# A graph network on one core: roots turned on TensorE, slots made early, a first strip by groups, and a loop of two blocks

## What is computed

```python
# part 1, over the edges (row = src, col = dst)
h = concatenate([x[row], x[col], edge_attr]) @ W1 + b1
h = relu((h - mean(h)) * rsqrt(var(h) + 1e-5) * gamma + beta)     # statistics over the edges
out = segment_sum(h @ W2 + b2, row) / (counts + 1) + x
x = layernorm(x + out)
# part 2
deg = segment_sum(1, dst with self loops);  dinv = rsqrt(deg);  norm = dinv[src] * dinv[dst]
conv = lambda h, W, b: segment_sum((h @ W)[src] * norm, dst) + b
h = relu(conv(x, W0, b0)); h = relu(conv(h, W1, b1))
x = layernorm(x + conv(h, W2, b2))
```

## Time and profile before

| | |
|---|---|
| median of 3 runs | 3832.4 us (3830.92 to 3836.69) |
| profiled execution | 3838.11 us, span 3836.3 us, mean granted clock 0.983 |
| TensorE busy | 3620.9 us (94%), matmuls x40721 |
| VectorE busy | 2525.0 us (66%) |
| ScalarE busy | 1489.2 us (39%) |
| GpSimd busy | 967.4 us (25%) |
| chain that ended last | PE 65%, DVE 24%, issue 8%, SPq 2%, ACT 1%, DMA 1% |

### The profile page before, as it was taken

One profiled execution on the slowest core, in us unless ns is written; L12 is line 12 of the kernel. 1 busy time (PEld: TensorE's weight loads), 2 busy tenths in 40 slices (PEclk: granted clock), 3 DMA queues, 4 the chain that ended last, 5 costly groups with the idle time before them and its releaser, 6 DMA issues.

```text
span 3836.3 us, 104225 instructions
## 1 busy us (share of the span) xinstructions
PE 3620.9 (94%) x40721; PEld 2589.0 (67%) x40942; DVE 2525.0 (66%) x3757; ACT 1489.2 (39%) x3772; POOL 967.4 (25%) x890
## 2 busy tenths in 40 slices
PE   4699999999998799999999999997999999999999
PEld 3488888888887677777777777774444444454444
DVE  6899999999995689888989889973111111111112
ACT  5355555455453366666666666662000000000000
POOL 0001000000101467766767677610000000000000
PEclk8899999999999999999999999998999999999999
DMA  7222322322334755555555555544666566656664
GB/s 239 55 88 84 102 86 84 102 87 84 100 88 146 125 162 158 157 155 151 161 158 157 147 158 158 157 137 153 193 200 195 193 195 200 193 189 208 209 209 132
DMA packets 435059, 571.31 MB, mean 149 GB/s; under 512 B 200059, under 2 KB 359684, under 8 KB 427940
## 3 DMA queue, kind: packets, MB, share of 16 engines
q1 hardware_dynamic: 403140, 510.29, 43.6%
q0 software_dynamic: 25088, 51.43, 5.0%
q10 hardware_dynamic: 6624, 6.42, 0.5%
HBM read 458.48 MB, written 109.53 MB: 148 GB/s over the span
## 4 chain that ended last, share of the span: by engine, by line
PE 65%; DVE 24%; issue 8%; SPq 2%; ACT 1%; DMA 1%; DVEq 0%; ACTq 0%
PE py L1654 30%; PE ph L1358 11%; PE pSum L1375 10%; DVE prod_raw L1145 8%; PE ph L1361 7%; DVE ring_raw L1118 6%; PE ph L1353 3%; DVE q L1154 1%; DVE q L1171 1%; DVE q L1167 1%; PE pY L854 1%; DVE q L1168 1%; DVE rank L1178 1%; DVE q L1173 1%; PE pbk L915 1%
## 5 line engine op out<-in xcount | busy, mean ns | idle before, releaser
L1308 POOL DMA_INDIRECT q<-pq_dram,chosen x784 | 851.4, 1086 | 405.3 <-ACT ph L1411 204.1
L1654 PE MATMUL py<-ring_raw,p 128*128 128x512 bf16 (+1 forms) x3822 | 784.7, 368 | 18.0 <-DVE dummy L1814 16.1
L1358 PE MATMUL ph<-p,prod_raw 128*128 (+1 forms) x7056 | 685.3, 220 | 22.7 <-DVE prod_raw L1501 12.2
L1654 PEld LDWEIGHTS py<-ring_raw,p 128*128 128x128 bf16 x3822 | 362.3, 98 | 432.1 <-DVE dummy L1814 16.5
L1358 PEld LDWEIGHTS ph<-p,prod_raw 128*128 128x128 bf16 x7056 | 493.7, 98 | 122.6 <-issue 4.8
L1418 ACT ACTIVATE x<-ph 128x512 bf16<-128x512 f32 x588 | 351.3, 597 | 464.6 <-PE ph L1361 334.6
L1361 PE MATMUL ph<-q,prod_raw 128*128 128x128 bf16 x4704 | 522.4, 220 | 0.0
L1375 PE MATMUL pSum<-x,ring_raw 128*128 128x384 bf16 x2401 | 500.4, 328 | 4.9 <-DVE x L1519 4.9
L854 PE MATMUL pY<-p,ring_raw 128*128 128x128 bf16 x7203 | 502.5, 219 | 0.3 <-issue 0.3
L1514 DVE SCALAR_TENSOR_TENSOR ring_raw<-ph,x 128x512 f32<-128x512 f32 x588 | 403.9, 687 | 132.5 <-ACT x L1418 126.5
L1830 DVE TENSOR_TENSOR yt<-py,dinv_row 128x512 f32<-128x512 f32 (+1 forms) x39 | 25.8, 661 | 696.6 <-PE py L1654 696.6
(11 more groups left out here) (334 smaller groups left out, 4372.5 us busy)
## 6 DMA issues: line engine op xcount, KB each, us to landing
ring_raw<-at_dram SPq DMA_DIRECT2D x252, 896.0 KB, 4.8
at_dram<-ring_raw SPq DMA_DIRECT2D x49, 1568.0 KB, 5.7
prod_raw<-lrow_dram SPq DMA_DIRECT2D x147, 384.0 KB
prod_raw<-lrow_dram SPq DMA_DIRECT2D x196, 256.0 KB
prod_raw<-lrow_dram SPq DMA_DIRECT2D x49, 416.0 KB
q<-pq_dram,chosen POOLq DMA_INDIRECT x784
arow_dram<-x SPq DMA_DIRECT2D x294, 36.8 KB
x<-arow_dram SPq DMA_DIRECT2D x147, 54.0 KB
```

Source lines behind the costliest of these rows:

```text
L1308: nc.gpsimd.indirect_dma_start(q_rows[i][:, k, :], None, pq_rows, bass.IndirectOffsetOnAxis(ap=chosen[u][:, i, k:k + 1], axis=0)).then_inc ...
L1358: last = nc.tensor.matmul(bank[:, k * P:(k + 1) * P], T[q][:, 0, at:at + P], p_b[:, :, m3, :].rearrange("p a d -> p (a d)"), start=False, ...
L1654: last = nc.tensor.matmul(py[par][:, 0:w], g3[c % 2][:, 7 * i + m, k, :], ring[i][:, 0:w // P, m, :], start=i == m == k == 0, stop=i == m ...
```

## The change

Four edits, all in stages two and three:

1. SyncE no longer writes `dinv_col` to DRAM element by element. TensorE transposes it (behind the statistics, after `dinv_made`) into `pSum[0]`, ScalarE copies that to `dinv_rows` behind the root of the variance (`dinv_kept`), and SyncE writes 49 rows of 512 B, now behind the three loads of x. TensorE waits for `dinv_kept` ahead of the first `sums`.
2. `quarter` is split into `targets` (L1501) and `slots` (L1508). The four `slots(0, k)` now stand ahead of VectorE's wait for `square_used`, the four `targets(0, k)` behind the bound.
3. Every strip takes its chunks in the order 4, 5, 0, 1, 2, 3, 6. TensorE begins the first strip when VectorE has read group 11 (`cg_taken` 12, the last in the py banks), and waits ahead of each chunk for the groups whose blocks it reads; `third` signals `node_done` for each group.
4. TensorE's source loop has 2 blocks in its body instead of 16.

```diff
+CHUNKS = (4, 5, 0, 1, 2, 3, 6)
@@ sp_2
                     for k in range(4):
                         quarter(0, k)
-                    put(sp, S["dinv_made"], 1)
-                    sp.dma_start(dinv_dram.rearrange("a (b p) -> p (a b)", p=P), dinv_col[:], ...).then_inc(S["dinv_out"], 16)
                     for u in range(3):
                         sp.dma_start(fl(xg[u][:]), t["xT"][:, u * 512:(u + 1) * 512]).then_inc(S["x_in"], 16)
+                    put(sp, S["dinv_kept"], 1)
+                    sp.dma_start(dinv_dram.rearrange("a (b p) -> (a b) p", p=P), dinv_rows[0:B, :]).then_inc(S["dinv_out"], 16)
@@ pe_2
                     nc.tensor.matmul(st[:, D:2 * D], ones_f[0:3, :], xs[0:3, D:2 * D], start=False, stop=True).then_inc(S["stats_made"], 1)
+                    pe.wait_ge(S["dinv_made"], 1)
+                    nc.tensor.transpose(pSum[0][0:B, 0:D], dinv_col[:], ident_f[:]).then_inc(S["dinv_turned"], 1)
@@ pe_2, sums
+                        if isinstance(b, int) and b == g == 0:
+                            pe.wait_ge(S["dinv_kept"], 1)
                         pe.wait_ge(S["z_low"], b * 13 + (g + 1))
@@ pe_2
-                    each_block(pe, one_block, 16)
+                    each_block(pe, one_block, 2)
@@ act_2
                     nc.scalar.activation(bt[1][:], bt[0][:], ACT.Sqrt).then_inc(S["bn_rooted"], 1)
+                    act.wait_ge(S["dinv_turned"], 1)
+                    nc.scalar.activation(dinv_rows[0:B, :], pSum[0][0:B, 0:D], ACT.Copy).then_inc(S["dinv_kept"], 1)
@@ dve_2
+                    def quarter(b, k):
+                        targets(b, k)
+                        slots(b, k)
...
+                    for k in range(4):
+                        slots(0, k)
                     dve.wait_ge(S["square_used"], 7)
@@ dve_2
                     for k in range(4):
-                        quarter(0, k)
+                        targets(0, k)
                     one_block(0, 0, False)
@@ sp_3, strip_loads
-                    for i in range(7):
-                        put(sp, S["chunk_used"], (j + 13 * c) * 7 + i + 1)
+                    for n, i in enumerate(CHUNKS):
+                        put(sp, S["chunk_used"], (j + 13 * c) * 7 + n + 1)
                         chunk(i, j, w)
@@ pe_3
-                pe.wait_ge(S["credits3"], 1)
+                pe.wait_ge(S["cg_taken"], 12)
@@ pe_3, strip
-                    for i in range(7):
+                    for at, i in enumerate(CHUNKS):
                         pe.wait_ge(a_in[i], (n + 1) * 16)
+                        if isinstance(j, int) and c == j == 0:
+                            pe.wait_ge(S["node_done"], (7 * i + 6) // 4 + 1)
...
-                        if i == 1 and has_tail:
+                        if at == 1 and has_tail:
                             tail(c, n - 1, 4)
                 for c in range(3):
-                    pe.wait_ge(S["g_taken"], 13 * c + 1)
+                    if c:
+                        pe.wait_ge(S["g_taken"], 13 * c + 1)
                     strip(c, 0, c % 2, STRIP, False)
@@ dve_3
                 def third(j):
...
-                    return V.tensor_tensor(g3[0][:, 4 * j:4 * j + nb, 2, :], gb[:, 0:nb, :], g3[0][:, 4 * j:4 * j + nb, 1, :], ALU.subtract)
+                    V.tensor_tensor(g3[0][:, 4 * j:4 * j + nb, 2, :], gb[:, 0:nb, :], g3[0][:, 4 * j:4 * j + nb, 1, :], ALU.subtract).then_inc(S["node_done"], 1)
...
-                last.then_inc(S["node_done"], 1)
-                dve.wait_ge(S["node_done"], 1)
+                dve.wait_ge(S["node_done"], 13)
```

More of the change, by code:

```diff
@@ L575, in build @@
         S.update({n: fit_sem(n) for n in """phase2 rows_set quad_summed dv2 moments_in squared square_used weighed stats_made bn_sqrt bn_rooted bound_ready credits t_ready hf_ready
-             mm_done z_hi z_res z_mid z_low sum_done sum_taken credits3 node_done dinv_made dinv_out dinv_in s_turned s_copied s_made cg_taken c_squared x1_made ga_made g_hi g_res g_mid x_rest0 x_rest1
+             mm_done z_hi z_res z_mid z_low sum_done sum_taken credits3 node_done dinv_made dinv_turned dinv_kept dinv_out dinv_in s_turned s_copied s_made cg_taken c_squared x1_made ga_made g_hi g_res g_mid x_rest0 x_rest1
              chunk_used y_taken yt_ready tail_done ln_ask ln_root out_ready out_sent dv3 root_b x_in bias_done g_taken rows_chosen q_put bank_open""".split()})
@@ L1228, in build @@
                 psq = [x1_free[:, u * 7 * D:(u + 1) * 7 * D].rearrange("p (j d) -> p j d", d=D) for u in range(2)]
-                s_raw = sb("s_raw", [P, D])
+                s_raw = sb("s_raw", [P, D]); dinv_rows = sb("dinv_rows", [P, D])
                 wvb = sb("wvb", [P, 4, D], BF16); neg_g = sb("neg_g", [P, D]); bt = [sb(f"bt{u}", [P, D]) for u in range(4)]
@@ L1462, in dve_2, with targets, slots @@
                     link(V.scalar_tensor_tensor(out=s_raw[:], in0=wa[:, 1, :], scalar=a2_all[:, 4:5], in1=qa[:], op0=ALU.mult, op1=ALU.add))
+                    def quarter(b, k):
+                        targets(b, k)
+                        slots(b, k)
+                    def targets(b, k):
+                        dve.wait_ge(t_in[k], b * T_IN[k] + T_IN[k])
+                        places = T[k].rearrange("p f s -> p (f s)")[:, 0:(QCELLS[k] + len(TCELLS[k])) * P]
+                        V.tensor_scalar(places, places, pid1[:, 0:1], None, ALU.is_equal).then_inc(S["t_ready"], 1)
+                    def slots(b, k):
+                        if not (isinstance(b, int) and b == 0):
+                            dve.wait_ge(S["sum_done"], b * 13 + (QUARTERS[k][1] - 13))
+                        dims = [P, PAIRS[k], P, 2]
+                        cols = slice(4 * QUARTERS[k][0], 4 * QUARTERS[k][0] + 2 * PAIRS[k])
+                        own = lo_all[:, b:b + 1, cols] if isinstance(b, int) else lo_all[:, bass.ds(b, 1), cols]
+                        own = own.rearrange("p a (g u) -> p (a g) u", u=2).unsqueeze(2)
+                        V.tensor_tensor(hotf[k], iota_lo[:].unsqueeze(1).to_broadcast(dims), own.to_broadcast(dims), ALU.is_equal).then_inc(S["hf_ready"], 1)
+                    for k in range(4):
+                        slots(0, k)
                     dve.wait_ge(S["square_used"], 7)
@@ L1496, in dve_2 @@
                     last.then_inc(S["bound_ready"], 1)
[L1498 to L1508, removed]
                     def left(b, g):
@@ L1599, in pool_3 @@
             def pool_3(pool):
-                pool.wait_ge(S["node_done"], 1)
+                pool.wait_ge(S["node_done"], 13)
             def pe_3(pe):
@@ L1654, in strip @@
                                 last = nc.tensor.matmul(py[par][:, 0:w], g3[c % 2][:, 7 * i + m, k, :], ring[i][:, 0:w // P, m, :],
-                                                        start=i == m == k == 0, stop=i == m == 6 and k == 2)
+                                                        start=at == m == k == 0, stop=at == m == 6 and k == 2)
                         last.then_inc(S["chunk_used"], 1)
-                        if i == 1 and has_tail:
+                        if at == 1 and has_tail:
                             tail(c, n - 1, 4)
                 for c in range(3):
-                    pe.wait_ge(S["g_taken"], 13 * c + 1)
+                    if c:
+                        pe.wait_ge(S["g_taken"], 13 * c + 1)
                     strip(c, 0, c % 2, STRIP, False)
@@ L1804, in dve_3 @@
                     if 0 <= s - 2:
-                        last = third(s - 2)
+                        third(s - 2)
                     if 0 <= s - 1 < 13:
                         scaled(s - 1)
-                last.then_inc(S["node_done"], 1)
-                dve.wait_ge(S["node_done"], 1)
+                dve.wait_ge(S["node_done"], 13)
                 dve.wait_ge(S["x1_made"], 13)
```

1 line of the change is left out of this document (removed).

## The result

The changed kernel takes 3801.8 us (median of 4 runs, 3801.6 to 3802.7) against 3832.0 us (3830.9 to 3836.7) for the kernel before, measured in turn: 30.2 us less, a ratio of 0.9919 with an interval of 0.9902 to 0.9936, so 0.8% faster. In a second session, with more runs of the kernel before, it was 3800.0 against 3835.0: 35.0 us less. The profiled execution took 3802.7 us (span 3800.8) where that of before took 3838.1 (3836.3), 35.4 us less.

What follows compares the result with a forecast made beforehand. TensorE was taken to bound the source loop and convolutions. 11.8 + 10.0 + 0 + 13.3 = 35.1 us, from the profiled 3838.1 to 3803.0 us, and from the median 3832.4 to 3797.3 us; range 3791 to 3812.

Steps and rivals of the forecast that it cites:

- Edit 1: TensorE's source loop, two blocks a turn instead of 16: two stalls go, jumps cost nothing, -11.8 us (to +5.9).
- Rival (a): TensorE's source loop: each of 23 jumps fetches code at 5.9 us, 136 us instead of 11.8, 3933 us; chance 0.06.
- Rival (b): TensorE's source loop: a jump costs 0.5 us or so, 11.5 us for 23, giving 3809 us; chance 0.10.
- Edit 2: Inverse roots turned on TensorE and written as rows: three idle gaps and half clock in block 0 go, -10.0 us.
- Rival (c): Block 0 of the source loop stays slow, code and gathered rows late in any first pass: 3807 us; chance 0.11.
- Edit 3: Slot one-hots moved ahead of VectorE's wait during the moments: 0 us, between 0 and -1.
- Edit 4: First convolution strip started by groups, right behind the last read of the py banks: -13.3 us, 11 to 15.
- Rival (d): First convolution strip: the early start does not overlap, a chunk or bank being late: 3810 us; chance 0.05.

Runs made afterwards that it cites:

- a0: The changed kernel run again unchanged, as base of the later runs: 3800.0 us against 3835.0 us for the kernel before (0.9910).
- a2: The changed kernel with 16 blocks again in the body of TensorE's source loop: 3813.1 us, 0.9944 of the kernel before.
- a3: The changed kernel with inverse roots written element by element again, but still behind the loads of x: 3810.2 us, 0.9936 of the kernel before.
- a4: The changed kernel with the slot one-hots of block 0 behind the bound again: 3801.4 us, 0.9914 of the kernel before.
- a5: The changed kernel with the strip's chunks in plain order 0 to 6, waits for groups kept: 3801.8 us, 0.9912 of the kernel before.
- a1: The changed kernel with 4 blocks in the body of TensorE's source loop: 3861.9 us, 1.0073 of the kernel before.
- b1: The changed kernel with two own PSUM banks for the node pass's odd groups and chunk order 4, 0, 1, 2, 3, 5, 6: 3798.1 us, 0.9903 of the kernel before.

## Why the prediction was right

**What bounds the kernel:** right. In the profiles, what was taken from TensorE's idle time in the last two stages came out of the span (the table above).

**Edit 1, -11.8:** measured -9.9, in the first profile and in the traces of the pair a0 and a2 alike (13 between their medians). The step from the empty instruction queue of stage one to "the new body stays too" held. The term that was off is the jump, taken at 0 of a range up to 0.77 us: it is 0.07 us, 1.8 us over 23. Rival (a), 3933 us, did not come, but it is a real mechanism one size away: with a body of four it cost 62 us. The rule of the Trainium skill that speaks for it ("Runtime: NRT & Kernel Launch", Instruction fetch mechanics: a taken branch outside the current pages forces a fetch, so kernels prefer full unrolling) does not describe a body of 82 KB here, which jumped 23 times with three packets fetched; its other figure there, room for 2048 instructions, agrees with a body of some 1220 matmuls and weight loads that stays, and with one of twice that which doesn't. Rival (b) is right in kind, with a seventh of its price.

**Edit 2, -10.0:** measured -10.03, by a sum of the three gaps of the earlier trace rows and of the half clock behind the last. Rival (c), that the first pass is slow anyway, fell: not one of the gaps is left, the 2.23 us of "issue" among them. The prediction put the gain down to held queue and crawling packets together; a3 parts them, 7.5 and 2.6. That the sum met the measurement to 0.03 us is luck: the stretch is 37.90 and 38.45 us in the two traces of the change.

**Edit 3, 0:** a4 bounds it by 1.4 us of noise, the trace by 0.3.

**Edit 4, -13.3:** measured -13.31. The start was predicted from the last read of the py banks, and is 0.05 us behind it. Rival (d) did not come. The prediction worked with the new order of chunks and gave it no price of its own; a5 shows that it has none.

**Sum and transfer.** The profiled execution was to be at 3803.0 and is at 3802.7, and that this is so close is luck: the jumps cost 1.8 us that the sum took at 0, and the source loop began 1.86 us earlier, which no edit was to bring. The start moves from one execution to the next with the same work ahead of it: 1278.88 in before, and 1273.42 to 1277.86 in six traces of kernels that are all alike up to there (the change twice, a1, a2, a5, b1). The profile of before is 1.0 above the latest of them; whether the edits move the start a little is not shown.

The median was to be at 3797.3 and is at 3801.8, inside the range but 4.5 us off. 1.8 of them are the jumps. Most of the rest is the last step, taking the 35.1 from the median of three runs: with 9 and 8 runs that kernel has medians of 3835.0 and 3834.3, 2.3 above 3832.4 on the mean. With both put right the sum is 3801.4, where the change has 3801.8 and, in a0, 3800.0.

Two sums of the prediction don't fit together. Its range, to 3812, is said to hold the forecast with its bounds, but the upper bound of edit 1, 17.7 us above the forecast, would be 3815. And the chances of the forecast, (b), (c) and (d) add up to 0.92, where it has 0.91. Neither bears on the result.

## What to carry to other kernels

Compare the code that a hardware loop holds with a loop in the same trace that fetches nothing: if it fits, a jump is nearly free (0.07 us here) and more unrolling brought nothing; if it doesn't, fewer jumps are better, and a smaller body that still won't fit is worse. The DMA of single elements cost less here by its packets (2.6 us) than by the loads that stood behind it in its queue and held up those of the next block (7.5), so look first for the place, then for the shape. Where a median of three runs and a profiled execution differ by as much as a term of the sum, make the sum against the profile and widen the range of the median by that difference.

## What the runs showed of the hardware

**Code that fits.** A body of an estimated 82 KB jumped 23 times with three packets fetched, one of 164 KB and one of 660 KB were fetched at each turn, at 5.1 to 6.5 us a jump, of which 3.55 (a1) and 3.79 us are idle time. At the jump of a1 shown, the clock behind it is at 0.50 for 2 us and at 0.71 for 2, which is 1.6 us more, and so the 5.1.

**The clock after the same idle time.** TensorE is idle for 1.95 us ahead of the first strip of the second and of the third convolution in every kernel here. Seven traces on this chip have 40.97 us for the piece that follows, both times. b1 has 42.65 at the second, and a3 has 43.78 and 43.87. Of the five traces on the slower chips four have 40.97 both times, and e0_before, the kernel before unchanged, has 42.65 and 42.27. First a3, then e0_before:

```profile
2994.63 43.78 PE L1671 MATMUL py<-ring_raw,g 128*128 128x512 bf16 x189 [1.95 <-DVE dummy L1859]
...
3393.16 42.65 PE L1654 MATMUL py<-ring_raw,g 128*128 128x512 bf16 x189 [1.95 <-DVE dummy L1842]
```

The granted clock is 1.00 over 2990 to 3000 us in the changed kernel and 0.68 in a3. The same gap thus sometimes brings the clock down from its upper level and sometimes doesn't, at up to 2.9 us a place. That is more than the slots, the order of the chunks and, by its median, b1 are worth. What decides it is open.

**One kernel took 9% longer on two other chips.** The kernel before has medians of 4194 to 4199 us there against 3834 to 3835, and 348 of the 367 us of span between e0_before and the kernel before lie between the first and the last running sum (1565.7 against 1217.3 us), where TensorE has unexplained gaps while GpSimd gathers. The cause is open. Where a small edit is measured matters as much as how often: on such a chip the 10 us of edit 2 could not be seen at all.
